# Hot matrices of a graph-aggregation kernel: one fused FP32 operation of two tensors against BF16 operations of one tensor and scalars, strip by strip

## What is computed

```python
mask = A != 0
rank = jnp.cumsum(mask.astype(jnp.int32), axis=1) - 1
m_i = jnp.where(num_nbr > T, jnp.ceil(num_nbr / K), 1)          # T = 5, K = 2
keep = mask & ~(mask & ((rank + 1) % m_i[:, None] == 0))
svals = jnp.sort(jnp.where(keep[:, :, None], x[None], big), axis=1)
for q in (0.25, 0.5, 0.75):
    idx = jnp.maximum(jnp.ceil(q * n_keep) - 1, 0)
    agg = agg + picked(svals, idx) / 3
agg = 0.5 * jnp.where(n_keep > 0, agg, 0) + 0.5 * x
out = agg @ W.T + b + x
```

## Time and profile before

| | |
|---|---|
| median of 3 runs | 162.98 us (162.6 to 163.2) |
| the profiled execution | 163.07 us |
| its span | 161.2 us |
| TensorE matmul, weight loads | 92.9 us (58%), 47.8 us (30%) |
| VectorE | 108.0 us (67%), 492 instructions |
| ScalarE | 99.7 us (62%) |
| GpSimd | 71.7 us (44%) |
| transfer queues busy | near all of the first 28 of 40 slices of the span |
| hot matrices (line 853) | 44 operations, 22.0 us |
| mean granted TensorE clock | 0.812 of full speed |

### The profile page before, as it was taken

The page is one execution under the profiler, slowest core; times in us unless marked ns, Lnnn a source line. Parts: engine busy times, 40 slices in busy tenths (PEclk is TensorE's granted clock), DMA queues, the critical chain, the costliest instruction groups (busy, mean ns, idle before and its releaser), DMA issues.

```text
span 161.2 us, 1965 instructions
## 1 busy us (share of the span) xinstructions
PE 92.9 (58%) x478; PEld 47.8 (30%) x479; DVE 108.0 (67%) x492; ACT 99.7 (62%) x93; POOL 71.7 (44%) x104
## 2 busy tenths in 40 slices
PE   0002917763095597017967059827399898665961
PEld 0000303321032142002322024402146685534441
DVE  1013285729762468899885867889879999999900
ACT  3077777777867777777767877477895353441021
POOL 7990000000477730277760087773785277360030
PEclk9999996999758569755599755985559999999696
DMA  5999999999999999999999999999710152302002
GB/s 161 428 426 429 423 433 429 433 422 429 423 416 413 418 424 420 425 420 421 415 417 417 429 426 410 413 430 395 274 44 12 51 145 80 95 14 67 2 4 71
DMA packets 9571, 49.99 MB, mean 310 GB/s; under 512 B 1715, under 2 KB 5307, under 8 KB 6230
## 3 DMA queue, kind: packets, MB, share of 16 engines
q1 hardware_dynamic: 7648, 47.71, 71.8%
q0 software_dynamic: 1760, 2.07, 4.3%
q10 hardware_dynamic: 150, 0.07, 0.2%
HBM read 49.61 MB, written 1.71 MB: 318 GB/s over the span
## 4 chain that ended last, share of the span: by engine, by line
DVE 42%; DMA 32%; PE 16%; issue 7%; ACT 1%; SPq 1%; DVEq 0%
DMA adj<-in_adj 32%; PE ps_w L609 10%; DVE hot L853 6%; DVE rec L864 4%; PE ps_w L766 3%; DVE merged L972 2%; DVE merged L970 2%; DVE quads_b L970 2%; DVE quads_b L972 2%; DVE rest L909 1%; DVE keys L913 1%; DVE order L1018 1%; DVE quads_a L972 1%; DVE top L892 1%; PE ps_out L701 1%
## 5 line engine op out<-in xcount | busy, mean ns | idle before, releaser
L485 ACT ACTIVATE sq<-adj 128x3328 bf16<-128x3328 int32 x26 | 77.4, 2977 | 32.0 <-DMA adj<-in_adj 32.0
L609 PE MATMUL ps_w<-sq,hot 128*128 128x416 bf16 x208 | 56.8, 431 | 3.0 <-DVE hot L853 2.9
L586 PE MATMUL ps_place<-classes,before 128*128 128x2 bf16 x26 | 4.8, 184 | 54.7 <-DVEq L842 54.5
L430 POOL DMA_INDIRECT gath_a<-in_table,idx_a x12 | 13.7, 1145 | 50.8 <-DVEq L929 48.1
L430 POOL DMA_INDIRECT gath_b<-in_table,idx_b x24 | 25.4, 1056 | 7.3 <-issue 7.3
L609 PEld LDWEIGHTS ps_w<-sq,hot 128*128 128x128 bf16 x208 | 20.3, 115 | 26.7 <-issue 15.6
L853 DVE SCALAR_TENSOR_TENSOR hot<-slot_code,ps_place,strip_unit 128x256 bf16<-128x256 f32 (+1 forms) x44 | 22.0, 535 | 8.8 <-PE ps_place L586 3.7
L430 POOL DMA_INDIRECT gath_s<-in_table,idx_s x16 | 17.7, 1109 | 11.6 <-DVE idx_s L917 7.4
L586 PEld LDWEIGHTS ps_place<-classes,before 128*128 128x128 bf16 x26 | 2.8, 106 | 63.9 <-DVEq L842 52.5
L838 DVE TENSOR_SCALAR classes<-meta 128x1 bf16<-128x1 bf16 x18 | 2.8, 155 | 26.6 <-ACT sq L485 26.0
L864 DVE MAX8 rec<-ps_w 128x8 f32<-128x208 f32 x32 | 9.7, 366 | 0.0
(11 more groups left out here) (244 smaller groups left out, 158.5 us busy)
## 6 DMA issues: line engine op xcount, KB each, us to landing
adj<-in_adj SPq DMA_DIRECT2D x26, 1664.0 KB, 12.4
out<-res SPq DMA_DIRECT2D x6, 192.0 KB, 2.0
xT<-in_xT SPq DMA_DIRECT2D x1, 896.0 KB, 17.5
xT<-in_xT SPq DMA_DIRECT2D x1, 768.0 KB, 15.4
gath_b<-in_table,idx_b POOLq DMA_INDIRECT x24, 6.1
gath_s<-in_table,idx_s POOLq DMA_INDIRECT x16, 2.8
out<-res SPq DMA_DIRECT2D x1, 256.0 KB, 2.3
out<-res SPq DMA_DIRECT2D x2, 128.0 KB, 2.3
```

Of the source, the lines that this page charges most:

```text
L430: nc.gpsimd.indirect_dma_start(slots[:, k, :], None, x_table, bass.IndirectOffsetOnAxis(ap=indices[:, k:k + 1], axis=0), bounds_check=TABL ...
L485: nc.scalar.activation(sq_ring[t % RING][:], adj_ring[t % RING][:], ACT.Square, accum_out=meta[:, t, 0:1]).then_inc(s_sq, 1)
L586: last = nc.tensor.matmul(ps_class[:, t, :], before[:], classes[:, t, :], start=(t == first), stop=True, skip_group_check=True)
L609: last = nc.tensor.matmul(ps_w[b % 2][h][:, 0:HW], hot[t % 3][:, s, :], sq_ring[t % RING][:, first:first + HW], start=False, stop=end and ...
```

## The change

slot_code becomes BF16 and OUT_OF_CLASS becomes 128 in place of 512, so that every slot code (-128 to -1) is whole in BF16. The hot matrix of a pair tile is made by two comparisons into strip 0 (64 columns each), a wait for the second of them, and three multiplications of strip 0 by 2, 4 and 8. The hot matrix of a tile alone is made by four operations, each a comparison and a multiplication by 2^k. Each of these operations reads one tensor and scalars; strip_unit and its four memsets go. The overflow test reads the class flags where it read the signs, so the operation that made `negative` goes.

```diff
-OUT_OF_CLASS = 512
+OUT_OF_CLASS = 128
-        slot_code = sb("slot_code", [P, P], F32)
+        slot_code = sb("slot_code", [P, P], BF16)
-            for k in range(STRIPS):
-                did(v.memset(strip_unit[:, k:k + 1], float(1 << k)))
                 at = hot[t % 3]
-                classed = 2 if block_of(t) < ALONE else 1
-                n = P // classed
-                for c in range(classed):
-                    part = slice(c * n, (c + 1) * n)
-                    last = v.scalar_tensor_tensor(
-                        out=at[:, :, part], in0=slot_code[:, 0:n].unsqueeze(1).broadcast_to([P, STRIPS, n]),
-                        scalar=ps_class[:, t, c:c + 1], in1=strip_unit[:].unsqueeze(2).broadcast_to([P, STRIPS, n]),
-                        op0=ALU.is_equal, op1=ALU.mult)
+                place = ps_class[:, t, :]
+                if block_of(t) < ALONE:
+                    for c in range(2):
+                        part = slice(c * HALF, (c + 1) * HALF)
+                        one = did(v.tensor_scalar(at[:, 0, part], slot_code[:, 0:HALF], place[:, c:c + 1], None,
+                                                  ALU.is_equal))
+                    need(one)
+                    for k in range(1, STRIPS):
+                        last = v.tensor_scalar(at[:, k, :], at[:, 0, :], float(1 << k), None, ALU.mult)
+                else:
+                    for k in range(STRIPS):
+                        last = v.tensor_scalar(at[:, k, :], slot_code[:], place[:, 0:1], float(1 << k), ALU.is_equal,
+                                               ALU.mult)
                 last.then_inc(s_hot, 1)
...
-            v.tensor_scalar(negative[:], ps_place[:, 0:2 * NT], 0.0, None, ALU.is_lt)
...
-                                   scalar=float(HALF - OUT_OF_CLASS), in1=signs[:, 0:first_alone, :],
+                                   scalar=float(HALF - OUT_OF_CLASS), in1=classes[:, 0:first_alone, :],
...
-                                       scalar=float(P - OUT_OF_CLASS), in1=signs[:, first_alone:NT, :],
+                                       scalar=float(P - OUT_OF_CLASS), in1=classes[:, first_alone:NT, :],
```

More of the change, by code:

```diff
@@ L117, in build @@
         classes = sb("classes", [P, NT, 2], BF16)
-        strip_unit = sb("strip_unit", [P, STRIPS], F32)
         hot = [sb(f"hot{i}", [P, STRIPS, P], BF16) for i in range(3)]
@@ L195, in build @@
         bad_t = sb("bad_t", [P, 2, NB], F32)
-        negative = sb("negative", [P, 2 * NT], F32)
         slow_sum = sb("slow_sum", [P, 1], F32)
@@ L1217, in _ @@
             bad_rows = bad[:, NB:].rearrange("p (t c) -> p t c", c=2)
-            signs = negative[:].rearrange("p (t c) -> p t c", c=2)
             low_high(pb[:, :, 0, :], pb[:, :, 1, :], pg[:, :, 0, :], pg[:, :, 1, :])
-            v.tensor_scalar(negative[:], ps_place[:, 0:2 * NT], 0.0, None, ALU.is_lt)
             did(v.scalar_tensor_tensor(out=bad_t[:, 0, :], in0=counts, scalar=6.0, in1=valid[:], op0=ALU.is_ge,
```

## The result

| | before | after |
|---|---|---|
| median, range, runs | 163.09 us (162.6 to 163.26), 4 | 165.65 us (165.4 to 166.28), 4 |
| ratio, 95% interval | | 1.0135 [1.0088, 1.0182] |
| profiled execution, span | 163.07, 161.2 us | 165.4, 163.6 us |
| slow_n begins | 147.77 | 148.66 |
| warm-up matmuls | 148.83, lasting 4.43 | 149.72, lasting 5.49 |

By the medians the changed kernel is slower by 2.56 us (1.6%). The prediction was 162.5 us, "same", with a range up to 164.2: wrong in sign, and out of its range. The experiments ran in four sets (e1 to e4, e5 to e8, e9 to e12, e13 to e16), each beside the kernel before on its own chip.

The account below looks back on a forecast made before the run. The adj transfer was taken to bind up to about 53 us, mainly VectorE from 61.3 us on. Gains 0.48 + 0.05 + 0.12 less 0.2 made 0.45 us: 162.98 to 162.5 us, range 161.6 to 164.2.

Parts of the forecast that it names:

- Intervals of the hot matrices: On VectorE, pair tile 0.72 us against 0.81, tile alone 0.65 against 0.67: gains of 0.48 and 0.05 us.
- rival (c): Hot matrices don't reach the fast rate at all, 1.05 ns a column: +3.9 us, 166.9 us; chance 0.04.
- (a): PSUM place scalar or two-scalar form drops hot-matrix comparisons to two columns per step: 163.4 us; chance 0.13.
- The sign operation: In the tail, the VectorE operation at 142.45 us goes: gain 0.12 us, kept up to slow_n.
- GpSimd beside it: Pair tiles 13 to 16, built beside gathers, end late at the new wait: 0.05 us each, 0.2 us.
- Rival (b): VectorE-GpSimd lock delays hot matrices of tiles 13 to 16 and 18 to 25: 163.9 us; chance 0.15.
- Where a gain on the chain reaches the end: VectorE work from tile 12 (61.29 us) on counts unless waits take it; 1.2 us gainable before squares bind.
- rival (d): No gather lateness (0.65 us gained), TensorE's clock rising sooner at 95 and 116 us: 161.6 us; chance 0.28.

Follow-up runs that it names:

- e1: Changed kernel with its hot matrices back in the old form (FP32, two tensors): 166.67 us (3 runs), ratio 1.0223 to the kernel before.
- e4: Kernel before with 73 covered one-column memsets added on VectorE at the start: 166.2 us in its only run that counts.
- e5: The changed kernel again, without further edits: 167.65 us (3 runs).
- e8: Changed kernel with the warm-up matmuls moved ahead of the wait for slow_n: 166.75 us (5 runs).
- e9: Kernel before with 22 warm-up matmuls ahead of the wait for slow_n and more in the tail's gaps: 163.13 us (4 runs), ratio 0.9932.
- e12: Kernel before with a GpSimd memset ahead of block 7's gathers: 165.26 us (4 runs), ratio 1.0082.
- e13: Changed kernel with 128 covered one-column memsets added on VectorE at the start: 165.63 us in one run.
- e16: Changed kernel with 127 covered VectorE memsets and TensorE fed by warm-up matmuls over the tail: 163.93 us (4 runs), ratio 1.0118.
- e14: Changed kernel with 127 covered one-column memsets added on VectorE at the start: 166.21 us in one run.

## Why the prediction was wrong

- **Intervals of the hot matrices**: right but for a little. Pair tile 0.75 for 0.72, tile alone 0.67 for 0.65, so the gain on six pair tiles is 6 x 0.06 = 0.36 at most for 0.48, and nothing for 0.05. The fast rate was reached, which refutes rival (c), and with a scalar in PSUM, which refutes (a): 64 columns and a multiplication more cost 8 ns (245 to 253), where two columns per step, 0.52 ns a column as in the spots operations of the earlier trace rows, would make it 33 for the columns alone. The Trainium skill's page "VectorE: DVE Perf Modes" (section "Why PSUM operands drop a tier") caps an operation with any PSUM operand at two columns per step; by lines 849 and 856 a scalar does not count as one.
- **The sign operation**: 0.12, right.
- **GpSimd beside it**: the 0.2 us was about right in size (two pair tiles of six lost their gain of 0.06, one of them 0.05 more), but placed wrongly. What cost time was the other direction: gathers stretched to 2.24 us, so that their result was waited for. Rival (b) put a price on 13 hot operations; none of them carried the loss. By the lock that the Trainium skill's page "SBUF — State Buffer" (section "SBUF: two separate sides") describes, either side can be held for a whole instruction of the other. A hot operation could then have waited for most of a gather, but none here lasted over 0.50 us; it was the gathers that lengthened, and no run here shows that the lock did it.
- **Where a gain on the chain reaches the end**: this step failed. The text took stalls, gathers and clock of the other 120 us as they stood and let the local gain run through them. But 73 more instructions moved every later instruction against fixed positions. That put a stall of 0.37 us at 112 us on the chain and another at pick, took one of 0.15 at 128.50 away from VectorE, and so set the gathers of gath_s 0.2 us later against it. Their last landing, 142.23 for 140.32 us, used up a slack of 0.93 that the text did not look for (it took the stream of squares as fixed too, and tile 20's ended 2.0 us later), and slow_n came 0.89 us later, where 0.4 to 0.7 sooner was forecast. The edits gave 0.2 on the pair tiles and 0.12 at the sign operation. They were costed by their durations, and by nothing for their number.
- **The clock**: rival (d) saw that clock steps are worth more than the edit, and looked for them at 95 and 116 us. They came at 149 to 160.7 and against the change: a lateness of 0.89 became 2.4 in the span. This tail had no term in the sum. The forecast's condition for being wrong ("the intervals come out as said and the end doesn't move with them") is what came.

Left open: why gathers lengthen, why adj falls behind with more instructions on VectorE, and how much of the 2.56 us belongs to each cause on another chip. The repeats scatter by up to 4 us, with TensorE instructions that start late by 1.3 and more. With stalls and clock both out of the way e16's ratio is 1.0118, with 1 just inside its interval, so a rest of the loss is neither shown nor excluded. e9's gain of 0.7% (0.06 to 1.3%) is measured for the kernel before only.

## What to carry to other kernels

Count what an edit adds in instructions, not only in microseconds. On an engine whose stream is on the chain, one instruction more or fewer can move a stall of 0.36 us onto or off a wait; whether that costs anything is read from what binds next behind it. Where the sum of an edit is below about a per cent, look first at what lies close behind it (a transfer that is barely in time, a clock step just after the last matmuls), because a few tenths there can turn into two microseconds either way. And if TensorE's clock matters at the end, feed it over the gaps: with the same slow_n that was worth 2.8 us here (e14 against e16), more than the edit could give.

## What the runs showed of the hardware that was not expected

- VectorE stalls for 0.35 to 0.37 us at fixed numbers of its recorded instructions, 128 apart (319, 447, 575, 703; 0.34 at 63, amid equal memsets), where nothing is queued ahead of them; one instruction more or fewer ahead moves it.
- A BF16 comparison of one tensor with a scalar in PSUM lasts 245 ns for 64 columns; with a multiplication added and 128 columns it lasts 253.
- The stream of adj runs later the more instructions VectorE has: squares of tile 20 within 0.1 us at 585 recorded instructions, 2.0 late at 658, 3.0 late at 785.
- Gathers on GpSimd, 1.00 us in most places, took 1.45 and 2.24 us beside 128x512 operations of VectorE that themselves kept their 0.67 us.
- The granted clock fell at about 158.5 us in both kernels, though the work was 1.95 us later in the second.
